# An audio tower on one core: the beta add of pairs 2 to 7 on the vector engine, with all instruction lists rewritten

## The reference

```python
# tok: depthwise conv of 3 taps, projection 64 -> 128, layer norm with g and b
x_mixed = einsum('btc,dc->btd', conv(x), lin_w) + lin_b + emb.mean(axis=0)
h = (x_mixed - mu) * rsqrt(var + 1e-5) * ln_g + ln_b          # ln_b is "beta" here
# attention on layernorm(h), one head of 128, with one row of A masked
QK = WQ @ WK^T;  c0 = argmin(sum(QK[0], axis=1))
h = h + where(row == c0, 0, softmax(QK / 8)) @ WV
# feed-forward over the 128 features: lower-triangular W1, gelu, lower-triangular W2
h = h + tril(W2) @ gelu(tril(W1) @ layernorm(h) + b1) + b2
```

## Time and profile before

| | before |
|---|---|
| time, median of 3 runs | 94.26 us (94.08 to 94.42) |
| time of the profiled execution | 93.75 us |
| its span, first to last instruction | 92.0 us |
| PE busy | 85.0 us (92%) |
| DVE busy | 73.6 us (80%) |
| ACT busy | 67.6 us (73%) |
| POOL busy | 54.9 us (60%) |

### The profile page before, as it was taken

One profiled execution on the slowest core, in us unless ns is written; L12 is line 12 of the kernel. 1 busy time (PEld: TensorE's weight loads), 2 busy tenths in 40 slices (PEclk: granted clock), 3 DMA queues, 4 the chain that ended last, 5 costly groups with the idle time before them and its releaser, 6 DMA issues.

```text
span 92.0 us, 1984 instructions
## 1 busy us (share of the span) xinstructions
PE 85.0 (92%) x541; PEld 69.5 (76%) x541; DVE 73.6 (80%) x283; ACT 67.6 (73%) x241; POOL 54.9 (60%) x89
## 2 busy tenths in 40 slices
PE   5979987699999999999999999999999999999940
PEld 2446565379799989999899899989887988687730
DVE  2259999998999998999998899869769395862560
ACT  1688999999999769969787988666796735555400
POOL 5508768898856793999982079972708437460000
PEclk9999999999999999999999999999999999999999
DMA  1986000000000000000000000000000003425364
GB/s 23 218 289 200 0 0 4 4 0 0 11 0 0 0 0 0 0 7 4 4 0 0 0 0 7 0 0 0 0 0 0 0 7 111 115 69 154 108 188 150
DMA packets 3828, 3.84 MB, mean 42 GB/s; under 512 B 413, under 2 KB 3690, under 8 KB 3818
## 3 DMA queue, kind: packets, MB, share of 16 engines
q1 hardware_dynamic: 3466, 3.35, 13.1%
q10 hardware_dynamic: 352, 0.38, 1.4%
...
## 4 chain that ended last, share of the span: by engine, by line
PE 72%; DVE 8%; POOL 8%; DMA 3%; issue 3%; ACT 1%; POOLq 0%; DVEq 0%
PE bank_m L400 14%; PE bank_s L373 12%; PE bank_o L411 8%; PE bank_s L431 7%; PE bank_at L391 7%; PE bank_np L364 6%; PE bank_np L444 4%; PE bank_x L422 4%; POOL rstd L207 4%; DMA tok_w<-tok_dram 3%; PE bank_np L356 3%; PE bank_at L444 3%; POOL rstd_x L198 2%; DVE hb_all L774 2%; DVE bn L688 1%
## 5 line engine op out<-in xcount | busy, mean ns | idle before, releaser
L373 PE MATMUL bank_s<-n1t,pt 128*125 128x250 f32 x64 | 16.0, 375 | 0.5 <-ACT pt L565 0.5
L400 PE MATMUL bank_m<-at,n 125*128 125x250 f32 x64 | 16.2, 374 | 0.0
L570 ACT ACTIVATE a<-bank_s,neg_max 125x250 f32<-125x250 f32 x32 | 15.1, 479 | 0.7 <-DVE neg_max L711 0.7
L222 POOL TENSOR_TENSOR hb_all<-h_all,rows_sb 125x512 f32<-125x512 f32 x8 | 10.2, 1272 | 4.0 <-DVE h_all L747 4.0
L711 DVE TENSOR_REDUCE neg_max<-bank_s 125x2 f32<-125x500 f32 x16 | 10.7, 670 | 2.1 <-PE bank_s L373 2.1
L373 PEld LDWEIGHTS bank_s<-n1t,pt 128*125 128x125 f32 x64 | 11.0, 187 | 1.6 <-issue 0.6
L400 PEld LDWEIGHTS bank_m<-at,n 125*128 125x128 f32 x64 | 11.2, 190 | 0.9
L577 ACT ACTIVATE at<-bank_at 125x500 f32<-125x500 f32 x16 | 9.6, 597 | 1.9 <-PE bank_at L391 1.9
L207 POOL TENSOR_TENSOR rstd<-var_eps,neg_half 125x4 f32<-125x4 f32 (+2 forms) x11 | 9.5, 863 | 1.9 <-DVE var_eps L700 0.6
L364 PE MATMUL bank_np<-n1t,qk_w 128*128 128x250 f32 x32 | 9.6, 381 | 0.6 <-ACT n1t L559 0.6
L747 DVE SCALAR_TENSOR_TENSOR h_all<-bank_o,rinv_keep,h_all 125x128 f32<-125x128 f32 x32 | 9.6, 343 | 0.2
...
## 6 DMA issues: line engine op xcount, KB each, us to landing
...
```

Source lines behind the costliest of these rows:

```text
L222: pool.tensor_tensor(hb_all[:, j, :, :], h_tiles[:, j, :, :], b2_4, ALU.add).then_inc(hb_ready, 1)
L373: last = nc.tensor.matmul(s_ps[b % 2][:, a, :], pt[b % DEEP][:, a * H:(a + 1) * H], n1t[b % DEEP][:, :], start=True, stop=True)
L400: last = nc.tensor.matmul(mix_ps, n1[b // 2 % (HELD // 2)][:, 2 * (b % 2) + c, :], at_sb[b % DEEP][:, c, :], start=(c == 0), stop=(c == 1))
L570: ins = nc.scalar.activation(a_sb[b % DEEP][:, a, :], s_ps[b % 2][:, a, :], ACT.Exp, bias=neg_max[b % 2][:, a:a + 1], accum_out=exp_sum[:, ...
```

## The change

`add_beta` goes from POOL's block to DVE's, with the same wait, the same operands and the same semaphore. So DVE issues six more 125x512 adds and POOL six fewer. The lists of all four engines are written anew: the same calls, in another order, with one number changed: the third `keep_warm` of PE is 9 and not 4. Below, the lists are cut to their beginnings.

```diff
@@ POOL
-            def add_beta(k):
-                pool.wait_ge(x_scaled, 4 * k + 4)
-                pool.tensor_tensor(h_tiles[:, k, :, :], scaled[k % 2][:, :, :], beta_4, ALU.add).then_inc(h_ready, 1)
-
...
-            keep_triangles(); root_x(1, 0, 2); root_x(1, 2, 2); root_1(0, 2, 2); root_1(1, 0, 2)
-            root_x(2, 0, 4); root_x(3, 0, 4); root_1(1, 2, 2); add_beta(2); add_beta(3); root_1(2, 0, 4)
...
+            root_x(0, 0, 1); root_x(0, 1, 1); root_x(0, 2, 2); root_x(1, 0, 2); root_1(0, 0, 1)
+            keep_triangles(); root_1(0, 1, 1); root_x(1, 2, 2); root_1(0, 2, 2); root_x(2, 0, 4)
+            root_1(1, 0, 2); root_x(3, 0, 4); root_1(1, 2, 2); root_1(2, 0, 4); root_x(4, 0, 4)
...
@@ PE
-            keep_warm(4)
-            wv_centre(); qk_centre(2)
+            keep_warm(9)
+            w1_centre(); qk_centre(2); project(2); wv_centre()
             pe.wait_ge(ident_ready, 1)
-            turn_n1_tile(0); turn_n1_tile(1); project(2); queries(0); w1_centre(); scores(0); turn_n1(1)
-            queries(1); row_sums(); turn_n1(2); scores(1); turn_a(0); queries(2); project(4); turn_n1(3)
-            scores(2); queries(3); turn_a(1); mix(0); turn_n1(4); scores(3); queries(4); mix(1); turn_a(2)
...
+            turn_n1_tile(0); turn_n1_tile(1); queries(0); turn_n1(1); scores(0); queries(1); turn_n1(2)
+            scores(1); queries(2); project(4); turn_n1(3); row_sums(); turn_a(0); queries(3); scores(2)
+            turn_a(1); turn_n1(4); scores(3); queries(4); mix(0); turn_n1(5); scores(4); attend(0)
...
@@ ACT
-            normalize_tile(1); out_qk(2); out_wv(); out_n1t(0); first_tap(5); add_tokens(); square(2, 0)
...
+            first_tap(5); normalize_tile(1); out_qk(2); first_tap(6); square(2, 0); square(2, 1)
+            square(2, 2); square(2, 3); out_n1t(0); normalize_1_head(1); square(3, 0); out_p(0)
...
@@ DVE
+            def add_beta(k):
+                dve.wait_ge(x_scaled, 4 * k + 4)
+                nc.vector.tensor_tensor(h_tiles[:, k, :, :], scaled[k % 2][:, :, :], beta_4, ALU.add).then_inc(h_ready, 1)
...
-            scale_x(2, 0, 4); scale_x(3, 0, 4); row_max(1); stats_1(2, 0, 4); aggregate_1(2, 0, 4)
-            least_sum(); candidates(); row_max(2); normalize_1(2); first_candidate(); stats_1(3, 0, 4)
...
+            scale_x(2, 0, 4); row_max(0); scale_x(3, 0, 4); add_beta(2); stats_1(2, 0, 4)
+            aggregate_1(2, 0, 4); row_max(1); add_beta(3); least_sum(); candidates(); normalize_1(2)
...
```

More of the change, by code:

```diff
@@ L462, in _ @@
[L462 to L471, removed]
@@ new lines, in _ @@
+            turn_a(1); turn_n1(4); scores(3); queries(4); mix(0); turn_n1(5); scores(4); attend(0)
+            turn_a(2); mix(1); queries(5); turn_a(3); mix(2); turn_n1(6); scores(5); attend(1); queries(6)
+            project(6); turn_n1(7); turn_a(4); scores(6); mix(3); queries(7); attend(2); turn_a(5)
+            turn_n1(8); mix(4); queries(8); attend(3); scores(7); turn_n1(9); mix(5); queries(9)
+            turn_a(6); scores(8); turn_n1(10); attend(4); scores(9); queries(10); turn_a(7); mix(6)
@@ new lines, in _ @@
+            turn_n1(11); attend(5); scores(10); turn_a(8); mix(7); queries(11); attend(6); mix(8)
+            turn_a(9); scores(11); turn_n1(12); turn_a(10); mix(9); queries(12); attend(7); turn_n2(0)
+            turn_n1(13); scores(12); mix(10); queries(13); attend(8); turn_a(11); turn_n1(14); scores(13)
+            attend(9); queries(14); mix(11); turn_n1(15); scores(14); turn_a(12); queries(15); turn_n2(1)
+            attend(10); scores(15); turn_a(13); attend(11); mix(12); up(0); mix(13); turn_a(14)
@@ L603, in _ @@
[L603 to L621, removed]
+            square(0, 2); square(0, 3); out_qk(0); first_tap(2); square(1, 0); square(1, 1); first_tap(3)
+            out_qk(1); first_tap(4); square(1, 2); square(1, 3); normalize_tile(0); bias_rows()
@@ new lines, in _ @@
+            first_tap(5); normalize_tile(1); out_qk(2); first_tap(6); square(2, 0); square(2, 1)
+            square(2, 2); square(2, 3); out_n1t(0); normalize_1_head(1); square(3, 0); out_p(0)
+            square(3, 1); square(3, 2); square(3, 3); out_n1t(1); add_tokens(); normalize_1_head(2)
+            out_p(1); first_tap(7); out_w1(); out_n1t(2); exps(0, 0); normalize_1_head(3); out_wv()
+            out_p(2); exps(0, 1); square(4, 0); out_n1t(3); exps(1, 0); exps(1, 1); out_at(0); out_p(3)
@@ new lines, in _ @@
+            square(4, 1); square(4, 2); square(4, 3); square(5, 0); out_n1t(4); exps(2, 0); exps(2, 1)
+            out_p(4); square(5, 1); square(5, 2); out_mix(0); out_at(1); out_n1t(5); square(5, 3)
+            exps(3, 0); exps(3, 1); out_at(2); out_mix(1); out_p(5); out_at(3); out_mix(2); out_n1t(6)
+            exps(4, 0); out_p(6); exps(4, 1); exps(5, 0); square(6, 0); square(6, 1); square(6, 2)
+            square(6, 3); square(7, 0); out_n1t(7); out_at(4); exps(5, 1); out_mix(3); out_p(7)
@@ L810, in _ @@
[L810 to L813 removed]
+            aggregate_1(0, 0, 1); second_tap(2); add_eps(0, 0, 1); stats_1(0, 1, 1); second_tap(3)
+            aggregate_1(0, 1, 1); third_tap(2); add_eps(0, 1, 1); scale_x(0, 2, 2); third_tap(3)
@@ new lines, in _ @@
+            first_candidate(); row_max(3); kept_rows(); second_tap(7); drop_row(0); third_tap(6)
+            third_tap(7); residual(0); scale_x(4, 0, 4); inverse_sums(1); normalize_1(3); scale_x(5, 0, 4)
+            row_max(4); add_beta(4); row_max(5); stats_1(4, 0, 4); stats_2(0); aggregate_1(4, 0, 4)
+            drop_row(1); add_beta(5); residual(1); stats_1(5, 0, 4); normalize_1(4); aggregate_1(5, 0, 4)
+            inverse_sums(2); drop_row(2); stats_2(1); residual(2); row_max(6); aggregate_2(0)
@@ new lines, in _ @@
+            scale_x(6, 0, 4); row_max(7); residual(3); normalize_1(5); add_beta(6); row_max(8)
+            residual(4); scale_x(7, 0, 4); row_max(9); inverse_sums(3); normalize_2(0); stats_1(6, 0, 4)
+            aggregate_1(6, 0, 4); drop_row(3); inverse_sums(4); residual(5); stats_2(2); row_max(10)
+            stats_2(3); residual(6); normalize_1(6); add_beta(7); stats_1(7, 0, 4); stats_2(4)
+            aggregate_1(7, 0, 4); row_max(11); aggregate_2(1); drop_row(4); residual(7); stats_2(5)
```

73 lines of the change are left out of this document (35 added, 38 removed).

## The result

The changed kernel takes 95.66 us (median of 4 runs, 95.28 to 98.13), where before takes 94.27 beside it: a ratio of 1.0136 [1.0102, 1.0171]. A second set of 11 runs gave 1.0098 [1.0067, 1.0128]. By the medians it is slower by 1.0 us in the second set and 1.4 in the first; the forecast was 95.4.

The account below looks back on a forecast made before the run. PE was taken to bound the kernel without a break from 24.92 us. Head 0.85 plus rest 0.3 gave 1.15 us, profiled 94.9 against 93.75; with the median 0.5 above, 95.4 us, range 94.8 to 96.2.

Parts of the forecast that it names:

- the head: Stretch up to the transpose turn_n1(4): that would start at 24.92 us, against 24.07 for equal work, 0.85 us slower.
- the rest: Behind turn_n1(4): PE catches up with DVE at three places, costing 0.3 us together, bounds 0 and 0.9.
- Step 1: Start of PE's list: w1_centre waits for POOL's triangles until 12.1 us, project(2) starts at 12.75; 0.3 us idle or more.
- Step 2: ACT puts four squares of pair 2 ahead of out_n1t(0): queries(0) at 15.5 against 13.72, scores(0) at 16.9 against 15.1.
- Step 3: Most lateness is made good in former PE idle time: project(4) at 20.5 us, against 20.55.
- Step 4: DVE's first adds, 0.61 us to the next start; turn_a(1) at 24.4, turn_n1(4) at 24.9 us.
- The marker: Event turn_n1(4), a PE transpose at 24.92 us before; with equal work left 24.07, any later start being the loss.
- The rival behind this term: DVE becomes the bound: adds charge PE between 28 and 54 us, 2.1 us slower, 96.4 us, bound 97.6; chance 0.15.
- POOL closed out: POOL roots starting in a DVE add wait; two tight places, at most 0.4 us each, 95.9 us; chance 0.08.
- The blocks on DVE: drop_row and two more DVE instructions, free of POOL's beta adds or add_b2, take about 1.2 us less.
- the head is not filled: Denies the rival that new lists fill 1.9 us of early PE idle: 0.8 us faster, 93.5 us, bound 92.4; chance 0.18.
- the losses do not cancel: Denies the rival that early PE and ACT delays are recovered by turn_n1(4): no change, 94.3 us; chance 0.14.

Follow-up runs that it names:

- w1_late: The changed kernel with the old start of PE's list in part: keep_warm(4), wv_centre ahead, w1_centre behind queries(0); median 95.5 us, ratio 1.0118.
- undo_move: The changed kernel with its new lists, but the six beta adds back on POOL; 95.95 us against 94.32, ratio 1.0177.
- adds_only: The kernel before with its old lists, only the six adds moved from POOL to DVE, each just ahead of its statistics; 96.08 us, ratio 1.0170.
- splice: Old lists up to about 20 us, then the changed kernel's lists with adds on DVE, mix(0) ahead of turn_n1(4); 95.75 us, ratio 1.0132.
- max_first: The changed kernel with row_max(1) back ahead of add_beta(2) and mix(0) back ahead of turn_n1(4); median 96.2 us, ratio 1.0179.
- tokens_late: The changed kernel with ACT's add_tokens moved from ahead of normalize_1_head(2) to behind out_p(1); median 95.3 us, ratio 1.0089.
- sums_early: The changed kernel with PE's row_sums moved ahead of turn_n1(2) and ACT's out_w1 ahead of add_tokens; median 95.5 us, ratio 1.0108.

## Why the prediction was right

The sign, the place and the mechanism hold: most of the loss lies in the head, and behind it the adds cost almost nothing. The forecast was 1.15 us; the split shows 0.86 + 0.07 = 0.93. The medians differ by 1.4 us in the first set and 1.0 in the second. I put what goes beyond 0.93 down to chance in the starts, which no run isolates. The head was forecast to 0.01 and the term for the rest 0.2 too large, so that the medians, 95.66 and 95.33, lie as near to 95.4 as they do in part by luck. Point by point, times brought to the frame of before by taking off the 0.67 of the start:

- **Step 1** had `w1_centre` at 12.1 and `project(2)` at 12.75, 0.3 later than before. Measured 11.82 and 12.53. POOL gates the first, as said, but the triangles take 0.54 us and not 0.73, so that there are 0.07 us of idle behind the nine products and not the 0.3 that were to show it; and this is not what delays `project(2)`: w1_late shows DVE's `third_tap(3)` there with the triangles out of the way. The term was mis-attributed and 0.2 too large.
- **Step 2** had `queries(0)` at 15.5 behind ACT's squares and `scores(0)` at 16.9. Measured 15.44, with a wait of 0.93 for ACT, and 16.90.
- **Step 3** had `turn_n1(2)` near 18.9, `scores(1)` at 19.15 and `project(4)` at 20.5. Measured 18.94, 19.18 and 20.54.
- **Step 4** had adds of 0.6 to 0.7 us and `turn_n1(4)` at 24.9. `out_at(0)` on ACT ends at 24.20, against 24.35. The timeline of DVE:

```profile
20.80 0.67 DVE L679 TENSOR_TENSOR h_all<-scaled,rows_sb 125x512 f32<-125x512 f32 x1
21.50 0.87 DVE L687 BATCH_NORM_STATS2 bn<-h_all 125x6 f32<-125x128 f32 x4
22.41 0.38 DVE L693 BATCH_NORM_AGGREGATE mv<-bn 125x2 f32<-125x6 f32 x4
22.71 0.65 DVE L710 TENSOR_REDUCE neg_max<-bank_s 125x2 f32<-125x500 f32 x1
23.27 0.68 DVE L679 TENSOR_TENSOR h_all<-scaled,rows_sb 125x512 f32<-125x512 f32 x1
...
24.38 0.48 DVE L719 SCALAR_TENSOR_TENSOR cand<-bank_o,least,token_row 125x250 f32<-125x250 f32 x1
24.85 0.69 DVE L705 TENSOR_TENSOR n<-h_all,rstd 125x512 f32<-125x512 f32 x1
```

The marker is at 24.93 in the frame of before, against 24.9. It was well chosen, for a reason that I had only in part: in both kernels DVE's `normalize_1(2)` starts at 24.17 or 24.18. Before has by then waited 0.36 us for POOL's add (its statistics start at 21.35) and has done `row_max(2)`; the changed kernel has made two adds instead. The list of PE that goes with it has `mix(0)` not done, 0.85 us. PE comes almost at the same moment, so that moving one engine frees little, but not quite: the marker's weight load waits 0.15 us for `normalize_1(2)` (timeline of PE's weight loads).

```profile
25.59 0.20 PEld L351 LDWEIGHTS bank_np<-ident,n 125*128 125x128 f32 x2 [0.15 <-DVE n L705]
```

The prediction had both at 24.9, PE behind `turn_a(1)` and DVE's multiplication. In the trace DVE is the later. `turn_a(1)` starts at 24.93, and such a group takes 0.53 us to the next start behind a wait (24.74 to 25.27 in undo_move), which would have let the marker start at 25.46.

- **The rest**, 0.3 with bounds 0 and 0.9, was 0.07 and 0.08, and PE's busy time from 20 to 60 us was 40.00, not below 39.85. The waits at `turn_n1(6)`, `turn_n1(8)` and `attend(3)` did not come. The lower bound was right; my walk over 20 us of lists added small errors and took their sum for waits. The rival behind this term is real with the old lists (adds_only).
- **POOL closed out**: real, on the path, and small. The rival had put up to 0.4 on each of two places. The root of pair 2 started at 23.28, 0.01 behind `add_beta(3)`, and took half as long again as the same root in before. POOL timelines, before and after:

```profile
23.12 1.02 POOL L207 TENSOR_TENSOR rstd<-var_eps,neg_half 125x4 f32<-125x4 f32 x1
```

```profile
23.28 1.54 POOL L207 TENSOR_TENSOR rstd<-var_eps,neg_half 125x4 f32<-125x4 f32 x1
```

The first ends at 24.14 and the second at 24.82, and `normalize_1(2)` starts 0.03 us behind each, at 24.17 and 24.85. It does so, by 0.02 to 0.04, in all 14 profiles of this study, and in ten of them the marker follows the end of `normalize_1(2)` by 0.05 or 0.06. So in these ten this root and the multiplication behind it release the marker. What the stretching costs is less than its 0.5 us, since DVE's own list is nearly as late: `candidates` starts at 24.38, and in before the next instruction starts 0.39 behind it (23.04 to 23.43), which would be 24.77. By this estimate from two rows, POOL closed out costs 0.08 of the 0.86. No run tests it by itself. By the rule of the Trainium skill that the prediction named (SBUF — State Buffer, Who interferes with whom), the trace agrees.

- **The blocks on DVE** were to give back 1.2 us, and DVE's busy time to come to about 76. It came to 78.0. The three slow `drop_row` of before are gone, but in the new lists other instructions meet POOL's `add_b2`: two `drop_row` of 1.06 and 1.23 us, at 63.85 and 73.83, and two `normalize_2` of 1.40 and 1.23, at 67.56 and 69.40. undo_move shows the same four (1.07 and 1.23, 1.39 and 1.23) and adds_only none of them, so they come of the new order and not of the move. PE does not feel them: the body is 0.07 longer.
- **From the profiled span to the median** I added 0.5 us, and the median was 95.66 in the first set and 95.3 in the second. The sum for the span, 93.15, lies between the two profiles, 92.9 and 93.6, which differ by the start alone.
- The other rivals fail: the head is not filled (PE works 12.75 of the 15 us from 10 to 25, before 13.10), and the losses do not cancel.

What stays open: why the products after 4 us become fast at varying moments, why the weights land late for PE in some executions, and whether a head exists that keeps the new body at the old marker; four tries (splice, max_first, tokens_late, sums_early) did not find one. No version tried here, with all six adds on DVE or one, beats the kernel before.
